# One core of a ViT tower: diagonal, projection and norm jobs re-cut, tree operands padded to 128 rows

## What is computed

```python
h = _L0_tok_ref(x, ...)                                  # selection, then a class token ahead
h = h + _L0_attn_ref(_layernorm(h), Wqkv, bqkv, W0, b0)
#   q, k, v = (x @ Wqkv + bqkv).reshape(3, b, n, 64, 8 heads)
#   attn = softmax(q k^T / 8, axis=1); av = diagonal of attn, times v; out = av @ W0 + b0
h = h + _L0_ffn_ref(_layernorm(h), ...)                  # GQA attention, RMS norms, experts
h = h + _L1_attn_ref(_layernorm(h), ...)                 # spectral filter
h = h + _L1_ffn_ref(_layernorm(h), w1s, b1s, w2s, b2s)
#   8 levels: score = x . w1s[node] + b1s[node]; node = 2*node + 1 + (score > 0)
#   out += gelu(|score|) * (x @ w2s[node] + b2s[node])
```

## Time and profile before

| what | us |
|---|---|
| median of 3 runs | 4308.63 (4298.92 to 4319.09) |
| the profiled execution, device time | 4311.47 |
| its span, first to last instruction | 4309.1 |
| attention turns (328.9 to 1884.0) | 1555.1 |
| first norm, n0 (238.1 to 280.4) | 42.3 |
| tree: set-up, scores, loop | 47.8, 117.1, 270.6 |
| PE, DVE, ACT, POOL busy | 3519.4, 2653.5, 2259.2, 696.7 |

### The profile page before, as it was taken

How to read it: one execution, slowest core, us unless ns; L and a number is a source line. 1 busy time by engine, 2 the same in 40 slices (tenths; PEclk the granted TensorE clock), 3 DMA queues, 4 the chain that set the end, 5 groups by cost and what they waited for, 6 DMA issues and landing times. The chain is left out here.

```text
span 4309.1 us, 60792 instructions
## 1 busy us (share of the span) xinstructions
PE 3519.4 (82%) x22648; PEld 1892.8 (44%) x22649; DVE 2653.5 (62%) x4431; ACT 2259.2 (52%) x4683; POOL 696.7 (16%) x693
## 2 busy tenths in 40 slices
PE   7549999999999999964888888759985997491896
PEld 6224444444444444332343434322224775271796
DVE  1617888887878888845877778324432333372575
ACT  1128888888888888943555555613331331120342
POOL 1310121111111111111000000024420001105443
PEclk7559999999999999986999999869997889655555
DMA  2031001111010010012000000153323122610112
GB/s 44 1 93 34 20 20 25 30 33 32 20 30 20 20 30 20 20 25 68 10 8 10 10 7 9 31 111 68 76 52 96 34 46 45 146 35 21 28 26 54
DMA packets 107095, 162.56 MB, mean 38 GB/s; under 512 B 66244, under 2 KB 89797, under 8 KB 98868
## 3 DMA queue, kind: packets, MB, share of 16 engines
q1 hardware_dynamic: 92188, 147.38, 15.5%
q0 software_dynamic: 5248, 5.71, 0.5%
q10 hardware_dynamic: 9393, 5.88, 0.4%
HBM read 85.15 MB, written 40.19 MB: 29 GB/s over the span
## 5 line engine op out<-in xcount | busy, mean ns | idle before, releaser
L970 DVE TENSOR_REDUCE att_NM<-att_ring 121x1 f32<-121x1024 f32 x1088 | 1251.4, 1214 | 315.6 <-PE att_ring L833 315.1
L905 ACT ACTIVATE att_ring<-att_ring,att_NM 121x1024 f32<-121x1024 f32 x1088 | 1193.8, 1123 | 115.4 <-DVE att_NM L970 114.8
L831 PE MATMUL att_ring<-att_q,att_k 64*121 64x512 f32 x2176 | 1166.6, 646 | 40.1 <-DVE att_Y L960 16.1
L833 PE MATMUL att_ring<-att_q,att_k 64*121 64x512 f32 x2176 | 1166.4, 646 | 0.0
L831 PEld LDWEIGHTS att_ring<-att_q,att_k 64*121 64x121 f32 x2176 | 346.2, 187 | 726.2 <-ACT att_ring L905 522.8
L1338 ACT ACTIVATE gqa_PT<-gqa_ring 121x484 f32<-121x484 f32 (+3 forms) x912 | 359.1, 450 | 197.7 <-PE gqa_ring L1265 131.9
L1382 DVE TENSOR_REDUCE gqa_NM<-gqa_ring 121x1 f32<-121x484 f32 (+1 forms) x720 | 374.8, 578 | 119.5 <-PE gqa_ring L1242 79.5
L833 PEld LDWEIGHTS att_ring<-att_q,att_k 64*121 64x121 f32 x2176 | 346.6, 187 | 0.0
L1265 PE MATMUL gqa_ring<-gqa_QS,gqa_KS 128*121 128x484 bf16 (+3 forms) x912 | 270.5, 327 | 35.9 <-ACT gqa_PT L1338 23.1
L1242 PE MATMUL gqa_ring<-gqa_KS,gqa_QS 128*121 128x484 bf16 (+1 forms) x720 | 252.6, 377 | 40.4 <-ACT gqa_PT L1338 19.1
L1722 DVE TENSOR_TENSOR moe_hh<-moe_sg,moe_p 128x484 f32<-128x484 f32 x204 | 134.2, 658 | 201.7 <-ACT moe_sg L1659 201.7
(11 more groups left out here) (439 smaller groups left out, 5505.2 us busy)
## 6 DMA issues: line engine op xcount, KB each, us to landing
moe_xw<-route_weights SPq DMA_DIRECT2D x17, 968.0 KB, 7.2
att_k<-att_k SPq DMA_DIRECT2D x32, 512.2 KB, 6.2
att_q<-att_q SPq DMA_DIRECT2D x32, 512.2 KB, 8.3
n_T<-h SPq DMA_DIRECT2D x16, 384.0 KB
by_freq<-stu_Yf SPq DMA_DIRECT2D x32, 160.0 KB
stu_YT<-by_freq SPq DMA_DIRECT2D x8, 640.0 KB, 5.6
moe_fs<-x_moe SPq DMA_DIRECT2D x4, 1028.5 KB, 11.1
sel_X<-in_x SPq DMA_DIRECT2D x4, 1024.0 KB
```

The source lines that it names most:

```text
L831: nc.tensor.matmul(to[0:TT, 0:512], lo[0:64, par, TT * t:TT * t + TT], mlo[0:64, par, CK * ck:CK * ck + 512], start=True, stop=True)
L833: nc.tensor.matmul(to[0:TT, 512:1024], hi[64:128, par, TT * t:TT * t + TT], mhi[64:128, par, CK * ck + 512:CK * ck + 1024], start=True, st ...
L905: nc.scalar.activation(to[0:TT, :], to[0:TT, :], ACT.Exp, bias=NM[0:TT, turn % 2, g, ck:ck + 1], accum_out=SS[0:TT, turn % 2, g, ck:ck + 1 ...
L970: nc.vector.tensor_reduce(NM[0:TT, turn % 2, g, ck:ck + 1], slot("score", turn, n)[0:TT, :], AX.X, ALU.max, negate=True).then_inc(S["max_r ...
```

## The change

**Norms.** Three means run ahead instead of one, in eight PSUM slots and three square buffers. ACT does Ln and Exp for chunks 0 to 5 and then for 6 to 10, and DVE finishes the first six chunks after the ninth centring. Loads and stores are six pieces of 768 columns.

**Attention.** A projection piece is split into 342 columns in rows 0 to 63 and 341 in rows 64 to 127, for which both x-pieces are loaded into both row halves; ACT moves out the first part and DVE the second. The diagonal is three jobs (6, 6 and 5 tiles) after scores 42, 46 and 50. The value jobs are five (4, 4, 4, 4 and 1 tiles) instead of three.

**Tree.** W1, WP, WG, xs and xT get 128 rows, of which rows 65 to 127 are zeros. POOL writes zeros into W1, xs and xT; SP fills WG and WP by 23 DMAs from a zero tile. SP waits for all nine of POOL's set-up steps before it loads the bias row.

```diff
@@ stage_norm
-    PARTS = 3
-    PW = 4 * CH
+    PARTS = 6
+    PW = 2 * CH
+    AHEAD = 3
+    HALVES = [(0, 6), (6, NC)]
...
-                    order += [("mean", k, 0)] if c == 0 else []
-                    order += [("mean", k, c + 1)] if c + 1 < NC else []
+                    order += [("mean", k, j) for j in range(AHEAD)] if c == 0 else []
+                    order += [("mean", k, c + AHEAD)] if c + AHEAD < NC else []
...
-                    if c == NC - 1:
-                        for t in range(s - NC + 1, s + 1):
+                    if c + 1 in (NC, HALVES[0][1] + AHEAD):
+                        c0, c1 = HALVES[0] if c + 1 < NC else HALVES[1]
+                        for t in range(s - c + c0, s - c + c1):
                             finish(t)
@@ stage_attn
-        VW_AT = {2 + 4 * j: j for j in range(NVW)}
-        PROJ_AT = {14 + 4 * j: NVW + j for j in range(NPR)}
-        SIDE_AT = {**VW_AT, **PROJ_AT, 44: DL}
-        TURN_AT = {50 + 5 * j: j for j in range(len(G))}
+        VW_AT = {2 + 3 * j: j for j in range(NVW)}
+        PROJ_AT = {18 + 4 * j: NVW + j for j in range(NPR)}
+        DL_AT = {42 + 4 * j: DL + j for j in range(NDL)}
+        SIDE_AT = {**VW_AT, **PROJ_AT, **DL_AT}
+        TURN_AT = {53 + 5 * j: j for j in range(len(G))}
...
-                    for o, w in ((0, 512), (512, M3 - 512)):
-                        ins = nc.tensor.matmul(pP[:, o:o + w], Wp[p, hp, c, :, :].rearrange("p h q -> p (h q)"), xqk[p, b % 2, o:o + w],
-                                               start=True, stop=True)
+                    for half, (o, w) in enumerate(SPANS):
+                        p = slice(64 * half, 64 * half + 64)
+                        ins = nc.tensor.matmul(pP[:, 512 * half:512 * half + w], Wp[p, hp, c, :, :].rearrange("p h q -> p (h q)"),
+                                               xqk[p, kind, b % 2, o:o + w], start=True, stop=True)
...
+                        if n in PROJ_AT and turn < NTURN - 1:
+                            j = PROJ_AT[n]
+                            dve.wait_ge(S["side_done"], own(turn, j))
+                            if j == NVW and turn > 0:
+                                dve.wait_ge(S["prod_ready"], 2 * (turn + 1))
+                            piece_half(turn + 1, j - NVW, slot("side", turn, j))
@@ stage_tree
-        WP = r.sb("WP", [65, PBASE[-1] + GROUPS, 2, 64])
-        WG = r.sb("WG", [65, GROUPS, 6, 64])
+        WP = r.sb("WP", [128, PBASE[-1] + GROUPS, 2, 64])
+        WG = r.sb("WG", [128, GROUPS, 6, 64])
...
+                sp.wait_ge(S["init"], NINIT)
                 sp.dma_start(W1[64:65, 0:NODES], b1s.rearrange("(a n) -> a n", a=1)).then_inc(S["loaded"], 16)
...
+                        for k in range(GROUPS // 2):
+                            sp.dma_start(WG[65:128, 2 * k:2 * k + 2, :, :].rearrange("p g n o -> p (g n o)"), Z0[0:63, 0:768]).then_inc(S["w2_loaded"], 16)
+                        for k in range(NPAIR // 6):
+                            sp.dma_start(WP[65:128, 6 * k:6 * k + 6, :, :].rearrange("p g n o -> p (g n o)"), Z0[0:63, 0:768]).then_inc(S["w2_loaded"], 16)
```

More of the change, by code:

```diff
@@ L647, in _ @@
                     sp.dma_start(W[p, :], wqkv).then_inc(S["w_loaded"], 16)
-                    sp.dma_start(xqk[p, 0, :], xsv[:, half, 0, :]).then_inc(S["staged"], 16)
+                    for kind in range(2):
+                        sp.dma_start(xqk[p, kind, 0, :], xsv[:, kind, 0, :]).then_inc(S["staged"], 16)
                 sp.dma_start(Brow[:, :], bqkv.rearrange("(c n) -> c n", c=3)).then_inc(S["w_loaded"], 16)
@@ L680, in _ @@
                         for half in range(2):
-                            sp.dma_start(xqk[64 * half:64 * half + 64, (b + 1) % 2, :], xsv[:, half, b + 1, :]).then_inc(S["staged"], 16)
+                            for kind in range(2):
+                                sp.dma_start(xqk[64 * half:64 * half + 64, kind, (b + 1) % 2, :], xsv[:, kind, b + 1, :]).then_inc(S["staged"], 16)
                         sp.dma_start(xv[0:64, (b + 1) % 2, PAD:PAD + M3], xsv[:, 2, b + 1, :]).then_inc(S["staged"], 16)
@@ L803, in side @@
                         pe.wait_ge(S["prod_ready"], 2 * (turn + 1))
-                        for t in range(NT):
+                        t0, nt = GD[j - DL]
+                        for t in range(t0, t0 + nt):
                             nc.tensor.matmul(pP[0:TT, 2 * t:2 * t + 2], pr[:, TT * t:TT * t + TT], halves[:, :], start=True, stop=True)
@@ L925, in _, with piece_half @@
                 dve.wait_ge(S["loaded"], 16 * (1 + 2 * HP))
+                def piece_half(turn, i, pP):
+                    hp, par, c = turn % HP, turn % 2, i // 2
+                    cols = slice(M3 * c + MH, M3 * c + M3)
+                    if i % 2 == 0:
+                        nc.vector.tensor_scalar(q[:, par, cols], pP[:, 512:512 + M3 - MH], float(D) ** -0.5, bq[:, hp, c:c + 1],
+                                                ALU.mult, ALU.add).then_inc(S["half_out"], 1)
+                    else:
+                        nc.vector.tensor_scalar(k[:, par, cols], pP[:, 512:512 + M3 - MH], bT[:, hp, c:c + 1], None, ALU.add).then_inc(S["half_out"], 1)
+                dve.wait_ge(S["wt_out"], 2)
+                for i in range(NPR):
+                    dve.wait_ge(S["side_done"], i + 1)
+                    piece_half(0, i, ring[:, 3, :])
                 def join(turn):
                     par = turn % 2
-                    dve.wait_ge(S["side_out"], own(turn, DL))
+                    dve.wait_ge(S["side_out"], own(turn, NSIDE - 1))
                     nc.vector.tensor_reduce(nM[0:TT, :], NM[0:TT, par, :, :], AX.X, ALU.min).then_inc(S["joined"], 1)
```

124 lines of the change are left out of this document (70 added, 54 removed).

## The result

The changed kernel takes 4193.88 us (median of 4 runs, 4186.22 to 4200.45), the kernel before 4311.39 us in the same series (4308.63, from which the forecast was taken, is the median of the first three of its four runs): a ratio of 0.973, with a 95% interval of 0.9703 to 0.9756. The forecast was 4133, the range 4080 to 4220. So it is faster, as forecast, and the time lies in the range, but 61 us above the likeliest value; of some 175 us expected, 117.5 came. The profiled execution (4186.22 us, span 4184.4) is the fastest of the four, so differences by stretch add up to 124.7 us.

What follows compares the result with a forecast made beforehand. DVE's maximum bounded the attention turns, waiting for PE; PE bounded the tree's loop. 4311.5 - 115 (attention) - 34 (norms) + 19.5 (tree set-up) - 43 (tree loop) - 3 (tree scores) = 4136, less 2.9 (median): 4133 us, range 4080 to 4220.

Steps and rivals of the forecast that it cites:

- Rival A: Tree: clock stays low because rows of zeros do no work; 43 + 3 us left out, 4179 us; chance 0.17.
- Rival C: Attention: three diagonal jobs hold the clock at 0.50 from score 42 to 54; slower, 4371 us; chance 0.03.
- Rival D: Attention: a projection piece on DVE costs 1 us instead of 0.42, waits included; 4187 us; chance 0.05.
- rival B: Attention: each diagonal job costs its own dry ring and clock fall, 9.9 us for 11; 4193 us; chance 0.08.
- PE's wait for chunk 2: Tree: PE waits for chunk 2 of xs behind SP's queue; 22.00 + 19.5 = 41.5 us forecast.
- Diagonal: Attention: three jobs leave 4.3 us of DVE idle on an empty score ring plus one clock fall; gain 5.2 a turn.
- Value jobs: Attention: half-size jobs hold PE half as long, so the wait mostly fits the ring; gain 1.4 us a turn.
- Projections and start: Attention: split projection pieces gain 0.5 us a turn, and 7 us ahead of turn 0.
- Norms: Five norms: means ahead, halved Ln/Exp and earlier stores gain 34 us, bounds 15 and 42.
- The rule that the prediction took from the Trainium skill: Norms: DVE with two SBUF inputs contends with GpSimd reading SBUF; 2.4 us more in each of four norms.
- The set-up: Tree: memsets, SP's later start and 23 zero DMAs (16.8 us) cost +19.5 us, bounds +15 and +26.
- The loop: Tree: zero rows raise PE's clock, DVE then bounds, a tile falls from 2.77 to 2.30 us; -43 us.

Runs made afterwards that it cites:

- norm_single: The changed kernel with ACT's two halves in the norms taken back (11 Ln, then 11 Exp, DVE multiplies after the last centring): 4195.32 us.

## Why the prediction was right or wrong

**Direction, and rivals.** Faster was right. Rival A (the tree's clock stays low) was wrong: 0.98 in the loop. Rival C (0.50 from the first job to the third) was wrong: 27 of the 29 low stretches of the clock beside the diagonal are over within 4 us. Rival D (a piece on DVE costs 1 us) was wrong: 0.48. The measured time is nearest to rival B's 4193, and part of its reason held (falls of the clock), but not its sum of 9.9 us a turn for three jobs: it was 8.2. Its 55 us for the attention come near the 52.9 + 6.0 = 58.9 measured by luck: the 1.7 us a turn that it gave the diagonal too little stand against the 1.8 that it, like the forecast, gave the value jobs too much. That the time lies in the range is owed to the range's width. The turns without turn-around jobs took 89 to 95 us and not 87 to 90, and PE's wait for chunk 2 was 53.66 us and not 41.5.

**Diagonal, the step that failed first.** Forecast was 4.3 us of dry ring and one fall of 1.5, 5.8 a turn. Measured were 3 x 1.87 = 5.6 and 31/16 = 1.9 falls of 3.2 - 1.87 = 1.3 us: 8.2. The sentence "I take one per turn" had no row behind it. The earlier trace rows showed a fall inside a job of 10 us and nothing on jobs of 2.5; the count, not the price, was the unknown, and it should have been carried as 0 to 3 a turn, 0 to 4.5 us. The bounds of 3 and 7 for the gain just held 3.2. The 11 us that stood before were right (11.4).

**Value jobs, the second step.** "The 1.23 us wait mostly fits into the ring" looked at one wait and the ring behind it, not at how soon the next job comes. Forecast +1.4 us a turn, measured -0.4; even the lower bound of 0 was on the wrong side. 1.8 x 16 = 29 us of the miss are here and 2.0 x 16 = 32 at the diagonal, 61 for the 55 by which the turns fell short (5 had been taken off the sum).

**Projections and start.** 0.4 us a turn for 0.5, and 6.0 us for 7.

**Norms.** 33.8 for 34, by errors against each other: n0, n4 and n5 gave 18.8 us together for 21.9, n3 6.2 for 3.5. "I reckon the last variance only 1.3 us earlier" was 0.2 in the changed kernel's n0 (26.9 us from its start to ACT's last Ln) and 5.8 in norm_single (21.3), against 27.1 in the kernel before, whose last Ln is this:

```profile
265.20 0.58 ACT L498 ACTIVATE n_R<-n_pS,n_eps 128x384 f32<-128x384 f32 x1 [1.30 <-PE n_pS L471]
```

So the three means ahead were worth more than was given them, and the halves took it back. The 3.2 us behind the last Ln did come (7.7 us from it to DVE's end in the kernel before, 4.9 in the changed one), but the halves hold that Ln up by 5.6. The draining after DVE's end was right: 271.9 - 267.15 = 4.75 for 4.7. The rule that the prediction took from the Trainium skill (SBUF — State Buffer, "Who interferes with whom") did not cost its 2.4 us in n0: the six early multiplications ran at 0.48 us each,

```profile
254.93 2.90 DVE L517 TENSOR_TENSOR n_T<-n_T,n_R 128x384 f32<-128x384 f32 x6 [2.47 <-ACT n_R L504]
```

since POOL's next squares wait for the centrings that are queued behind them. In n1, where POOL's squares do run beside DVE, five took 4.32 us,

```profile
1869.96 4.32 DVE L517 TENSOR_TENSOR n_T<-n_T,n_R 128x384 f32<-128x384 f32 x5 [5.97 <-ACT n_R L504]
```

0.86 each, which agrees with the rule as the earlier trace rows did.

**Tree.** The mechanisms were right, two sizes were off by some 10 us each in opposite directions. The set-up cost 28.8 for 19.5: the zeros took 0.94 each, above both bounds (0.64 and 0.9), 4.8 us more than the 16.8, and the loads behind them landed 4.7 us late, which no term held. The loop gave 56.6 for 43: I took a tile from 2.77 to 2.30, but the loop's mean tile was 269.9/96 = 2.81 before, and DVE's chain is 2.17 (2.22 on average).
